# Two deformable-attention stages of one kernel rearranged: x placed by ScalarE, two-tap spreads from tap 12, ten accumulating DMAs, hats of one direction each

## The chip, the core and the metric

The kernel runs on one core of a Trainium2 chip. The time is device microseconds of one execution. The core has five engines that run their own instruction lists and wait for each other on semaphores: TensorE (PE, matmuls; its weight loads are PEld), VectorE (DVE), ScalarE (ACT), GpSimd (POOL) and SyncE (SP, which only issues DMAs here). ACT and POOL issue DMAs too, as ACTq and POOLq.

## What is computed

The input x is 4 images of 64 channels and 32x32 pixels, f32. The first part is deformable attention with 8 heads of 4 points. Each pixel has, for each head and point, an offset (two projections of x) and a weight (a softmax over the head's 4 points of a third projection). The projected values are sampled bilinearly at the shifted place, weighted, summed, projected and added to x:

```
q = x as tokens;  v = q @ W_value + b_value
off = q @ W_off + b_off;  attn = softmax(q @ W_attn + b_attn) over the points
loc = pixel + off;  sampled = bilinear(v, loc)            (0 outside the image)
x = sum over points(sampled * attn) @ W_out + b_out + q
```

The second part is a binary 3x3 convolution on the sign of x, a batch norm over the whole batch, a residual sum and a PReLU:

```
y = conv3x3(sign(x + move0), scale * sign(conv_w))
y = batchnorm(y) * gamma + beta + x + move1
out = where(y >= 0, y, a * y) + move2
```

## The kernel before

**Layout.** Two images of 64 channels fill the 128 partitions, so the four images are two groups g (`G` = 2). The pixels are split into an upper and a lower half, `yh` = 0 and 1, of 512 pixels (`HALF`). The attention works at a fixed grid of 4x4 integer shifts of the value image, the taps. Tap t of 0 to 31 is one shift in one half: taps 0 to 15 are the upper half, 16 to 31 the lower, and four taps with one y shift are a row. The order of the shifts is `ORDER`. (Where an offset reaches beyond the grid, a flag sends the engines to a general branch at the end; it isn't taken with these inputs.)

**Weights of a tap.** For every tap the weight of a pixel is attention times a hat in y times a hat in x, where a hat is relu(1 - |position - shift|). ScalarE makes the positions `u` (L644) from PSUM, then for each shift the distances `tab` (`distances`, L651) and the hats `hat` (`hats`, L656), in 8 steps n listed in `HATS`; one step has both directions, 1024 elements. VectorE multiplies attention, turned by TensorE into `ps_att`, with the y hat of a row: `attend(n)` (L862), into a ring `ays`. POOL multiplies that with the x hat for each tap: `weight(t)` (L785), into the ring `ap` of `RAP` = 4. Only taps 0 and 1 have it done by VectorE (L871).

**Spread, product, unit.** TensorE copies the weights of a tap's heads to the channels, `spread(t)`: one tap at a time up to tap 15 (L461), 8 instructions, and from `FIRST_PAIR` = 16 on two taps on half the rows each (L466), 16 instructions a pair. In a pair the second tap's output lands in swapped quadrants, and it is multiplied with `vswap`, a copy of the values `vpad` with swapped partitions, made by two DMAs on SP (L390). VectorE multiplies with the shifted values: `product(t)` (L888), into the ring `prod` of `PR` = 12. TensorE projects a product with W_out and accumulates it in `ps_out`: `project(unit)` (L490), 8 instructions. Two products can be added first by an accumulating DMA that POOL issues (`sum_products`, L792); `SUM_FROM` says which, e.g. 4: 5 means that product 5 is added onto product 4, and both are then one unit. It is issued four taps behind in POOL's order. There are 8 such sums, so 24 units. When a unit is projected is written out in `TAPS_AFTER` (after which spread which taps) and `TAPS_AT_END`. After the upper units (`UPPER_UNITS`) ScalarE reads `ps_out` (L706, L707) and the lower half uses the same banks.

**x itself** is added by matmuls with the identity into `ps_out` ahead of the units of each half: `carry_x(yh)` (L483). The second also holds the sum for the flag (L477).

**Softmax.** It runs in three parts: two halves of the upper pixels (parts 0 and 1) and all lower pixels (part 2): logits on TensorE (L429), `softmax_max`, `softmax_sub`, exponentials on ScalarE, `softmax_sum`, `softmax_recip` on VectorE, and the scale `prob`, for part 2 on POOL (L803) behind tap 7. `turn(1)` transposes it and only then can rows of the lower half be attended. On VectorE these steps stand between products; `ROW_AFTER` says after which products the rows 1 to 7 are attended.

**Start.** SP and ACT load x's upper half (one group each), then SP `win` (the projections) and ACT `prm` (biases, positions). SP waits for `win` and x and issues `cst` (hats' shifts, identity, selectors), the lower x, and the rest. TensorE runs three warm-up matmuls (L542), then biases of the logits (L419) and base positions (L408), which need `prm`, then logits (L429), offsets (L412) and values (L438).

**End.** After the last spread come the units at the end, with part of the convolution between (`convolve_above`, L524), the signs (L713), the rest of the convolution, the batch norm (L995 to L1016) and the stores.

## Time and profile before

| | |
|---|---|
| median of 3 runs | 95.33 us (94.48 to 97.89) |
| the profiled execution | 94.7 us, of which the span of the profile is 92.9 us |
| PE busy | 74.7 us (80% of the span) |
| DVE busy | 62.6 us (67%) |
| POOL busy | 51.7 us (56%) |
| ACT busy | 44.4 us (48%) |
| mean granted TensorE clock | 0.949 of full speed |

The span is from the first to the last instruction that the profiler recorded; 1.8 us of the execution lie outside it. Busy time of PE is the time in which at least one matmul runs, and matmuls overlap, so the duration of a group in the timeline is a little longer than the step to the next. The chain of waits gives those steps. A count (x8) is of instructions: an f32 matmul shows as two.

### The profile page before, as it was taken

To read this page: it belongs to the slowest core of one execution; us is meant where nothing else is said; L and a number is where in the kernel's file an instruction comes from. 1 tells how busy PE (TensorE), PEld (TensorE's weight loads), DVE (VectorE), ACT (ScalarE), POOL (GpSimd) and SP (SyncE) were. 2 spreads that over 40 slices of the span, in tenths; PEclk is the share of its full clock that TensorE was granted. 3 is DMA by queue.
4 is the path that set the end of the run, shared out by engine and by line. 5 is a ranking of instruction groups with operands and counts; after the bars stand their busy time and mean duration, and the time that the engine had idled before them with its cause. 6 is when DMAs were issued, how large, how long until landed. Compare 5 with 4: busy or idle time off the path is not lost.

```text
span 92.9 us, 1673 instructions
## 1 busy us (share of the span) xinstructions
PE 74.7 (80%) x642; PEld 30.2 (32%) x642; DVE 62.6 (67%) x85; ACT 44.4 (48%) x71; POOL 51.7 (56%) x48
## 2 busy tenths in 40 slices
PE   5669999669999999999999999969999999210000
PEld 4257529112335743333321313201313455010000
DVE  2000997993799874999897969799624007659930
ACT  2200399996399999970000799000000039419900
POOL 7920000019998999999999999999600000006000
PEclk9999999999999999999999999999999999995555
DMA  1839800000049938073290190697740000000085
GB/s 34 275 77 276 312 3 0 0 0 7 0 85 210 236 70 169 7 153 72 48 178 11 28 196 9 125 185 148 141 85 0 0 7 0 0 0 0 11 259 185
DMA packets 3641, 8.37 MB, mean 90 GB/s; under 512 B 560, under 2 KB 1072, under 8 KB 3632
## 3 DMA queue, kind: packets, MB, share of 16 engines
q0 software_dynamic: 1152, 4.19, 23.8%
q1 hardware_dynamic: 2192, 3.76, 13.7%
q10 hardware_dynamic: 288, 0.30, 1.1%
q8 instruction: 5, 0.08, 0.3%
q14 instruction: 4, 0.03, 0.1%
HBM read 2.27 MB, written 1.05 MB: 36 GB/s over the span
## 4 chain that ended last, share of the span: by engine, by line
PE 69%; DVE 9%; ACT 6%; DMA 4%; POOL 4%; issue 2%; ACTq 1%; POOLq 0%; DVEq 0%
PE banks L490 23%; PE banks L461 13%; PE banks L466 10%; DMA prm<-params_dram 4%; PE banks L412 4%; PE banks L483 4%; PE banks L419 3%; PE banks L524 3%; PE banks L429 3%; POOL ap L785 2%; ACT prod L765 2%; PE banks L438 2%; PE banks L408 2%; ACT prod L767 2%; DVE a L871 1%
## 5 line engine op out<-in xcount | busy, mean ns | idle before, releaser
L785 POOL TENSOR_TENSOR ap<-ays,hat 128x512 f32<-128x512 f32 x30 | 41.0, 1589 | 15.3 <-ACT hat L656 15.3
L888 DVE TENSOR_TENSOR prod<-banks,vpad 128x1024 f32<-128x1024 f32 (+1 forms) x26 | 30.2, 1175 | 9.1 <-PE banks L461 4.6
L490 PE MATMUL banks<-prod,wo 64*64 64x512 f32 x192 | 24.6, 598 | 0.2 <-PE banks L490 0.2
L461 PE MATMUL banks<-ap,cst 64*64 64x512 f32 x112 | 15.1, 593 | 0.0
L466 PE MATMUL banks<-ap,cst 32*64 32x512 f32 x128 | 12.1, 612 | 0.9 <-POOL ap L785 0.7
L490 PEld LDWEIGHTS banks<-prod,wo 64*64 64x64 f32 x192 | 7.6, 132 | 13.6 <-issue 11.5
L811 POOL TENSOR_SCALAR prod<-prod,prm,st 128x512 f32<-128x512 f32 x2 | 1.5, 767 | 18.0 <-ACT st L759 18.0
L713 ACT ACTIVATE sg<-banks,st 128x512 bf16<-128x512 f32 x2 | 1.3, 690 | 17.7 <-PE banks L490 17.7
L651 ACT ACTIVATE tab<-u,cst 128x1024 f32<-128x1024 f32 x8 | 8.9, 1141 | 0.2
L792 POOL DMA_DIRECT2D prod<-prod x8 | 8.6, 1078 | 0.1
L888 DVE TENSOR_TENSOR prod<-banks,vswap 128x1024 f32<-128x1024 f32 x7 | 8.5, 1215 | 0.0
L656 ACT ACTIVATE hat<-tab 128x1024 f32<-128x1024 f32 x8 | 8.2, 1048 | 0.1
L461 PEld LDWEIGHTS banks<-ap,cst 64*64 64x64 f32 x112 | 4.8, 132 | 7.6 <-issue 4.0
L466 PEld LDWEIGHTS banks<-ap,cst 32*64 32x64 f32 x128 | 2.7, 130 | 9.7 <-POOL ap L785 5.4
L862 DVE TENSOR_TENSOR ays<-banks,hat 128x512 f32<-128x512 f32 x8 | 5.4, 680 | 0.6 <-PE banks L446 0.6
L706 ACT ACTIVATE x1n<-banks,prm 128x512 f32<-128x512 f32 x1 | 0.7, 690 | 10.0 <-PE banks L490 10.0
L670 ACT ACTIVATE ex<-lsub 128x256 f32<-128x256 f32 (+1 forms) x3 | 1.5, 485 | 7.8 <-DVE lsub L826 7.8
L524 PE MATMUL banks<-sg,wcb 64*64 64x512 bf16 (+2 forms) x84 | 4.6, 350 | 0.2 <-ACT sg L713 0.2
L929 DVE TENSOR_SCALAR x<-banks,prm 128x512 f32<-128x512 f32 x1 | 0.8, 750 | 5.7 <-ACT sg L713 5.7
L429 PEld LDWEIGHTS banks<-win,xs 128*128 128x128 f32 x32 | 4.2, 201 | 0.9 <-issue 0.8
L419 PE MATMUL banks<-prm,top_ones 128*128 128x256 f32 (+1 forms) x6 | 3.2, 660 | 1.5 <-DMA prm<-params_dram 1.5
L820 DVE TENSOR_REDUCE lmax<-banks 128x64 f32<-128x256 f32 (+1 forms) x3 | 1.5, 510 | 3.8 <-PE banks L429 3.8
(83 smaller groups left out, 86.3 us busy)
## 6 DMA issues: line engine op xcount, KB each, us to landing
prod<-prod POOLq DMA_DIRECT2D x8, 512.0 KB, 4.9
xs<-x_dram SPq DMA_DIRECT2D x3, 256.0 KB, 4.0
vswap<-vpad SPq DMA_DIRECT2D x2, 361.0 KB, 5.6
out_dram<-prod SPq DMA_DIRECT2D x4, 128.0 KB, 2.5
out_dram<-prod SPq DMA_DIRECT2D x2, 256.0 KB, 2.5
wcf<-w_conv_dram SPq DMA_DIRECT2D x1, 288.0 KB, 4.1
wab<-w_abs_dram SPq DMA_DIRECT2D x1, 288.0 KB, 4.2
xs<-x_dram ACTq DMA_DIRECT2D x1, 256.0 KB, 3.4
```

Source lines behind the costliest of these rows:

```text
L419: pe.matmul(ps_log[part][:, first:end], top_ones[:], prm[:, p_att:p_att + HP].unsqueeze(1).to_broadcast([P, (end - first) // HP, HP]), sta ...
L429: mm = pe.matmul(ps_log[part][:, at:at + C], xs[:, g, q:q + P], wp[:, 2, :], start=False, stop=((n + 1) * P == end and g == G - 1), skip_g ...
L461: mm = pe.matmul(spread_into(t)[rows_out, g, :], sel_of(g)[rows_in, rows_out], weights_at(t)[rows_in], start=True, stop=True)
L466: mm = pe.matmul(spread_into(t)[quadrant(i, g, t in SWAPPED)[1], g, :], sel_of(g)[rows_in, quadrant(i, g)[1]], weights_at(t)[rows_in], sta ...
L490: mm = pe.matmul(ps_out[g][rows_out], wo[rows_in, rows_in], source[rows_in, g, :], start=False, stop=last, skip_group_check=True)
L524: mm = pe.matmul(ps_y[yh][g][rows_out, first_row * W:last_row * W], wcb[rows_in, ky * K + kx, :], sg[rows_in, g, y0:y0 + last_row - first_ ...
L651: nc.scalar.activation(tab[:, n % 2], u[:, :, yh, :], ACT.Abs, bias=cst[:, c_tap + k:c_tap + k + 1]).then_inc(s_abs, 1)
L656: nc.scalar.activation(hat[:, yh, :, k, :], tab[:, n % 2], ACT.Relu, bias=1.0, scale=-1.0).then_inc(s_hat, 1)
L785: pool.tensor_tensor(ap[:, j % RAP, :], ays[:, t // TAPS % RY, :], hat[:, yh, 0, kx, :], ALU.mult).then_inc(s_ap, 1)
L792: pool.dma_start(prod[:, into % PR], prod[:, more % PR], accum_op=ALU.add).then_inc(s_s2[k % len(s_s2)], 16)
L862: nc.vector.tensor_tensor(ays[:, n % RY, :], ps_att[:], hat[:, yh, 1, ORDER[row], :], ALU.mult).then_inc(s_ay, 1)
L888: nc.vector.tensor_tensor(by_half_row(prod[:, t % PR, g, :]), by_half_row(spread_into(t)[:, g, :]), v_window(t, g), ALU.mult).then_inc(s_p, 1)
```

## The change

- TensorE no longer adds x. ScalarE copies x into `ps_out` ahead of each half's units (`place_x`, four instructions of 512 elements); the sum for the flag is a step of its own behind the last units but one (`sum_flag`), and its ScalarE step stands just ahead of the last signs.
- Spreads of two taps begin at tap 12 instead of 16, so taps 13 and 15 use `vswap`; that copy is made in two halves, the first as soon as the upper values are there.
- Ten sums instead of eight. In the first three rows second onto first and fourth onto third product (0: 1, 2: 3, and so on), row 3 has none; the lower half is unchanged. They are issued five taps behind instead of four. Units are 22 instead of 24, and `TAPS_AFTER` is written anew.
- `distances` and `hats` work on one direction each, in 16 steps of 512 elements, in the order y of row 0, all x, the other y; `tab` has 4 places.
- `prm` is SP's first issue, `win` ACT's second. The y positions are projected first.
- The ring `ap` has 6 places instead of 4. Attention of the two halves has a bank each, and other banks are dealt out anew (`ps_log`, `ps_flag`, `ps_y`), which takes some waits away; TensorE's offsets of the lower half are split over the places behind tap 1 and tap 2, values behind tap 4, `turn(1)` behind tap 6.
- VectorE attends rows after products 0, 2, 4, 7, 8, 9, 10 and does `softmax_sum(2)` and `softmax_recip(2)` behind products 2 and 3. POOL's `prob` stands behind tap 5 instead of tap 7.

The core of the diff:

```diff
-FIRST_PAIR = NT
+FIRST_PAIR = 12
 SPREADS = [(t,) for t in range(FIRST_PAIR)] + [(t, t + 1) for t in range(FIRST_PAIR, LAST - 1, 2)] + [(LAST - 1,), (LAST,)]
 SWAPPED = [taps[1] for taps in SPREADS if len(taps) == 2]
-SUM_FROM = {0: 1, 4: 5, 8: 9, 12: 13, 16: 18, 20: 22, 21: 23, 24: 26}
+SUM_FROM = {0: 1, 2: 3, 4: 5, 6: 7, 8: 9, 10: 11, 16: 18, 20: 22, 21: 23, 24: 26}
+SUM_BEHIND = 5
 DVE_COLUMNS = [2] + [0] * (ROWS - 1)
 GPSIMD_LINES = (0, 1)
 ORDER = (1, 0, 2, 3)
-HATS = [(yh, k) for yh in range(YH) for k in ORDER]
+POSITIONS = [(yh, d) for yh in range(YH) for d in (1, 0)]
+HATS = [(0, 1, ORDER[0])] + [(0, 0, k) for k in ORDER] + [(0, 1, k) for k in ORDER[1:]]
+HATS += [(1, d, k) for d in (1, 0) for k in ORDER]
 VP = H + TAPS
 HW = W // 2
...
-        tab = sb("tab", [P, 2, 2, HALF])
+        tab = sb("tab", [P, 4, HALF])
...
-        RA, RAP = 3, 4
+        RA, RAP = 3, 6
...
-        ps_att = bank[6]
-        ps_y = [[bank[0], bank[1]], [bank[2], bank[3]]]
+        ps_att = [bank[6], bank[7]]
+        ps_y = [[bank[2], bank[3]], [bank[6], bank[7]]]
         ps_v = [[bank[0], bank[1]], [bank[5], bank[4]]]
...
-        ps_log = [bank[7], bank[6], bank[4]]
-        ps_flag = bank[4]
+        ps_log = [bank[7], bank[6], bank[7]]
+        ps_flag = bank[6]
...
-        def wait_for_hat(engine, yh, k):
-            engine.wait_ge(s_hat, HATS.index((yh, k)) + 1)
+        def wait_for_hat(engine, yh, d, k):
+            engine.wait_ge(s_hat, HATS.index((yh, d, k)) + 1)
...
-        TAPS_AFTER = {6: [2, 3], 7: [0], 8: [6], 9: [7], 10: [4], 12: [10], 13: [11], 14: [8], 17: [14, 15], 19: [12],
-                      23: [17, 19], 25: [16], 29: [20], 30: [21, 25], 31: [27, 29]}
+        TAPS_AFTER = {7: [0], 8: [2], 11: [4], 13: [6], 15: [8, 12], 17: [10, 14, 13, 15], 21: [17, 19],
+                      25: [16], 27: [25], 29: [20], 30: [21, 27], 31: [29]}
         TAPS_AT_END = [24, 28, 30, 31]
         UNITS_AFTER = {t: [unit_of(k) for k in TAPS_AFTER[t]] for t in TAPS_AFTER}
         UNITS_AT_END = [unit_of(t) for t in TAPS_AT_END]
         UNITS = [unit for t in UNITS_AFTER for unit in UNITS_AFTER[t]] + UNITS_AT_END
-        UPPER_UNITS = UNITS.index(unit_of(12)) + 1
...
         @block.sync
         def _(sp):
+            sp.dma_start(prm[:], params).then_inc(s_prm, 16)
             sp.dma_start(chunk(xs, 1, 0), chunk_of(x, 1, 0)).then_inc(s_x[0], 16)
-            sp.dma_start(win[:], w_in).then_inc(s_win, 16)
             sp.wait_ge(s_win, 16)
             sp.wait_ge(s_x[0], 32)
             sp.dma_start(cst[:, 0:c_avg], const[:, 0:c_avg]).then_inc(s_cst, 16)
...
-            sp.wait_ge(s_vp, 2)
-            sp.wait_ge(s_vlow, 2)
-            for i in range(PAIR):
-                rows_in, rows_out = quadrant(i, 1)
-                sp.dma_start(vswap[rows_out, :, RH + 1:], vpad[rows_in, :, RH + 1:]).then_inc(s_vswap, 16)
+            for yh in range(YH):
+                sp.wait_ge([s_vp, s_vlow][yh], 2)
+                at = slice(yh * VP // YH, (yh + 1) * VP // YH)
+                for i in range(PAIR):
+                    rows_in, rows_out = quadrant(i, 1)
+                    sp.dma_start(vswap[rows_out, :, at], vpad[rows_in, :, at]).then_inc(s_vswap[yh], 16)
...
-                        pe.wait_ge(s_f1, 1)
-                    for i in range(PAIR):
-                        rows_of_i = slice(i * C, (i + 1) * C)
-                        mm = pe.matmul(ps_out[g][rows_of_i], cst[rows_of_i, c_eye + i * C:c_eye + (i + 1) * C],
-                                       chunk(xs, g, yh)[rows_of_i], start=True, stop=False, skip_group_check=True)
-                mm.then_inc(s_carry, 1)
+            def sum_flag():
+
+                pe.wait_ge(s_ov, 4)
+                pe.wait_ge(s_p, products_done(LAST - 1, G - 1))
+                pe.matmul(ps_flag[0:1, 0:4], ones[:, 0:1], over_sum[:], start=True, stop=True).then_inc(s_fps, 1)
...
-                    pe.wait_ge(s_carry, 1)
+                    pe.wait_ge(s_xin, G)
                 if unit == UNITS[UPPER_UNITS]:
-                    pe.wait_ge(s_carry, 2)
+                    pe.wait_ge(s_xin, 2 * G)
                 last = unit in (UNITS[UPPER_UNITS - 1], UNITS[-1])
                 if kind == "sum":
                     wait_for_sum(pe, n)
...
             pe.wait_ge(s_x[0], 32)
             logits(0, range(NCH // 2))
             logits(1, range(NCH // 2, NCH))
+            offsets(0, 1)
             offsets(0, 0)
-            offsets(0, 1)
             values(0)
+            pe.wait_ge(s_sub, 2)
+            logits_bias(2)
             pe.wait_ge(s_x[1], 32)
-            pe.wait_ge(s_u, 2)
-            logits_bias(2)
             logits(2, range(NCH // 2))
             pe.wait_ge(s_cst, 16)
-            pe.wait_ge(s_sub, 2)
             turn(0)
             logits(2, range(NCH // 2, NCH))
+            pe.wait_ge(s_u, 2)
+            base_positions(1, 1)
             for taps in SPREADS:
                 for t in taps:
                     spread(t)
                 if t == 1:
-                    pe.wait_ge(s_sub, 3)
-                    for d in reversed(range(2)):
-                        base_positions(1, d)
-                        offsets(1, d)
-                if t == 3:
+                    offsets(1, 1)
+                if t == 2:
+                    base_positions(1, 0)
+                    offsets(1, 0)
+                if t == 4:
                     pe.wait_ge(s_u, 4)
                     values(1)
-                if t == TAPS + 1:
-                    carry_x(0)
-                if t == 2 * TAPS:
-                    pe.wait_ge(s_ay, TAPS)
+                if t == 6:
                     turn(1)
-                if t == FIRST_PAIR + 5:
-                    carry_x(1)
                 for unit in UNITS_AFTER.get(t, []):
                     project(unit)
             for unit in UNITS_AT_END[:-1]:
                 project(unit)
+            sum_flag()
             pe.wait_ge(s_p, products_done(LAST - 2, G - 1))
...
             pe.wait_ge(s_p, products_done(NT * YH - 1, G - 1))
+            pe.wait_ge(s_f1, 1)
             pe.wait_ge(s_sg, 4)
...
             act.dma_start(chunk(xs, 0, 0), chunk_of(x, 0, 0)).then_inc(s_x[0], 16)
-            act.dma_start(prm[:], params).then_inc(s_prm, 16)
-
...
             def distances(n):
-                yh, k = HATS[n]
-                act.wait_ge(s_u, 2 * yh + 2)
-                if n >= 2:
-                    act.wait_ge(s_hat, n - 1)
-                nc.scalar.activation(tab[:, n % 2], u[:, :, yh, :], ACT.Abs, bias=cst[:, c_tap + k:c_tap + k + 1]).then_inc(s_abs, 1)
+                yh, d, k = HATS[n]
+                act.wait_ge(s_u, POSITIONS.index((yh, d)) + 1)
+                if n >= 4:
+                    act.wait_ge(s_hat, n - 3)
+                nc.scalar.activation(tab[:, n % 4], u[:, d, yh, :], ACT.Abs, bias=cst[:, c_tap + k:c_tap + k + 1]).then_inc(s_abs, 1)
 
             def hats(n):
-                yh, k = HATS[n]
+                yh, d, k = HATS[n]
                 act.wait_ge(s_abs, n + 1)
-                nc.scalar.activation(hat[:, yh, :, k, :], tab[:, n % 2], ACT.Relu, bias=1.0, scale=-1.0).then_inc(s_hat, 1)
+                nc.scalar.activation(hat[:, yh, d, k, :], tab[:, n % 4], ACT.Relu, bias=1.0, scale=-1.0).then_inc(s_hat, 1)
+
+            def two_hats(n):
+                distances(n)
+                distances(n + 1)
+                hats(n)
+                hats(n + 1)
+
+            def place_x(g, yh):
+                nc.scalar.activation(ps_out[g][:], chunk(xs, g, yh), ACT.Identity).then_inc(s_xin, 1)
...
-            positions(0, 0, 1)
-            positions(0, 1, 2)
+            positions(0, 1)
+            positions(0, 0)
             act.wait_ge(s_cst, 16)
             distances(0)
+            distances(1)
             hats(0)
-            distances(1)
+            distances(2)
             hats(1)
-            distances(2)
-            distances(3)
             hats(2)
-            hats(3)
-            positions(1, 1, 3)
-            positions(1, 0, 4)
+            two_hats(3)
+            two_hats(5)
             exponentials(2)
+            positions(1, 1)
+            positions(1, 0)
+            distances(7)
+            hats(7)
             act.wait_ge(s_zero, 2)
             act.wait_ge(s_v, 2)
             for g in range(G):
                 nc.scalar.activation(values_of(g, 1), both_halves(ps_v[1][g][:]), ACT.Identity,
                                      bias=prm[:, p_bv:p_bv + 1]).then_inc(s_vlow, 1)
-            distances(4)
-            hats(4)
-            distances(5)
-            distances(6)
-            hats(5)
-            distances(7)
-            hats(6)
-            hats(7)
+            for g in reversed(range(G)):
+                act.wait_ge(s_vlow, G - g)
+                place_x(g, 0)
+            for n in range(8, len(HATS), 2):
+                two_hats(n)
             for n in range(2 * YH):
...
             nc.scalar.activation(chunk(x1, 0, 0), ps_out[0][:], ACT.Identity, bias=prm[:, p_bo:p_bo + 1]).then_inc(s_x1, 1)
-            act.wait_ge(s_fps, 1)
-            nc.scalar.activation(flag[:, 4:8], ps_flag[0:1, 0:4], ACT.Identity, accum_out=flag[:, 0:1]).then_inc(s_f1, 1)
+            act.wait_ge(s_x1, 2)
+            for g in reversed(range(G)):
+                place_x(g, 1)
...
+            act.wait_ge(s_fps, 1)
+            nc.scalar.activation(flag[:, 4:8], ps_flag[0:1, 0:4], ACT.Identity, accum_out=flag[:, 0:1]).then_inc(s_f1, 1)
...
             for t in range(TAPS, NT * YH):
                 weight(t)
                 for into in SUM_FROM:
-                    if SUM_FROM[into] == t - TAPS:
+                    if SUM_FROM[into] == t - SUM_BEHIND:
                         sum_products(into)
-                if t == 2 * TAPS - 1:
+                if t == TAPS + 1:
                     pool.wait_ge(s_rec, 3)
                     pool.tensor_tensor(grouped(prob[:, 1, :]), grouped(ex[:, 1, :]), spread_points(lrec[:, 1, :]),
                                        ALU.mult).then_inc(s_prob, 1)
...
-                wait_for_hat(dve, yh, ORDER[row])
-                nc.vector.tensor_tensor(ays[:, n % RY, :], ps_att[:], hat[:, yh, 1, ORDER[row], :], ALU.mult).then_inc(s_ay, 1)
+                wait_for_hat(dve, yh, 1, ORDER[row])
...
                 if t in SWAPPED:
-                    dve.wait_ge(s_vswap, 16 * PAIR)
+                    for half in range(YH):
+                        dve.wait_ge(s_vswap[half], 16 * PAIR)
...
             weight(0)
+            weight(1)
             softmax_max(2)
-            weight(1)
-            ROW_AFTER = [1, 3, 5, 9, 10, 12, 13]
+            ROW_AFTER = [0, 2, 4, 7, 8, 9, 10]
             for t in range(NT * YH):
                 product(t)
                 if t == 0:
                     softmax_sub(2)
+                if t == 2:
+                    softmax_sum(2)
                 if t == 3:
-                    softmax_sum(2)
-                if t == 4:
                     softmax_recip(2)
                 if t in ROW_AFTER:
                     n = ROW_AFTER.index(t) + 1

```

## Rows read from the trace of the kernel before

**Rows 1.** Chain of waits, start to 58.9 us: start, duration, engine, tile, line, instructions

```profile
1.17 4.14 DMA prm<-params_dram
...
5.44 2.05 PE banks L419 x4
7.49 0.85 PE banks L408 x2
8.34 1.83 PE banks L429 x16
10.17 1.87 PE banks L412 x8
...
13.05 1.06 PE banks L419 x2
...
22.67 1.88 PE banks L461 x16
...
58.86 0.04 POOLq L784
```

**Rows 2.** Busy time by stretch; after each engine (instructions); then clock, DMA share, GB/s

```profile
12.00:15.00 3.00, 3.00 (x22) 1.70 (x21) 2.83 (x7) 2.88 (x4) 0.00 (x0) 1.00 0.00 0
...
20.00:60.00 40.00, 40.00 (x356) 14.03 (x360) 33.32 (x34) 24.83 (x44) 38.94 (x35) 1.00 0.45 91
```

**Rows 3.** Timeline of POOL: start, duration, engine, line, operation, tiles, count, idle before

```profile
20.48 2.51 POOL L785 TENSOR_TENSOR ap<-ays,hat 128x512 f32<-128x512 f32 x2 [15.26 <-ACT hat L656]
...
29.37 1.10 POOL L803 TENSOR_TENSOR prob<-ex,lrec 128x512 f32<-128x512 f32 x1 [0.43 <-DVE lrec L839]
...
62.42 1.98 POOL L785 TENSOR_TENSOR ap<-ays,hat 128x512 f32<-128x512 f32 x1
63.64 1.60 POOL L792 DMA_DIRECT2D prod<-prod  x1
64.25 2.29 POOL L785 TENSOR_TENSOR ap<-ays,hat 128x512 f32<-128x512 f32 x1
```

**Rows 4.** Chain of waits, TensorE from 27 us to its last unit

```profile
27.35 1.72 PE banks L483 x8
...
39.26 1.72 PE banks L461 x16
...
49.13 1.04 PE banks L466 x16
...
52.86 1.86 PE banks L483 x8
...
66.35 1.88 PE banks L490 x16
...
71.31 2.81 PE banks L490 x24
...
75.69 0.02 issue
```

**Rows 5.** Timeline of TensorE, its first instructions

```profile
0.99 2.93 PE L542 MATMUL banks<-ones 128*128 128x256 f32 x6 [0.99 <-POOL ones L773]
```

**Rows 6.** Timeline of ScalarE: positions of the upper half, and the upper result

```profile
11.56 1.27 ACT L644 ACTIVATE u<-banks,prm 128x512 f32<-128x512 f32 x2
...
51.26 0.69 ACT L706 ACTIVATE x1n<-banks,prm 128x512 f32<-128x512 f32 x1 [10.04 <-PE banks L490]
```

**Rows 7.** Timeline of VectorE in the first rows

```profile
19.80 1.21 DVE L888 TENSOR_TENSOR prod<-banks,vpad 128x1024 f32<-128x1024 f32 x1
20.93 0.68 DVE L862 TENSOR_TENSOR ays<-banks,hat 128x512 f32<-128x512 f32 x1
...
28.35 0.94 DVE L839 RECIPROCAL lrec<-lsum 128x128 f32<-128x128 f32 x1
```

**Rows 8.** Accumulating DMA, issue to landing; then the stores to DRAM, last their us

```profile
DMA to landing us min/median/max: 4.6/4.9/5.7
...
out_dram<-prod SPq DMA_DIRECT2D x2, 256.0 KB, 2.5
```

26 lines of the change are left out of this document (10 added, 16 removed).

## The prediction

> **What bounds the kernel now.** I read the chain of waits first. It begins with the wait for `prm`, the last of four early transfers, and only then come TensorE's bias and position matmuls [rows 1]. From 22.7 to 58.9 us the chain is TensorE without a break [rows 1], so a reader may think that every matmul taken away is gained. The stretches by engine correct this: between 20 and 60 us PE is busy 40.00 of 40 us, but POOL 38.94 too [rows 2]. The timeline of POOL shows why it is no less a bound. Its products of weights (`weight`, L785) start every 1.23 us (two take 2.51 from 20.48, one 1.28), with no idle time noted but 15.26 us before the first, where it waits for a hat, and 0.43 before `prob` [rows 3]. Near the end the completions of taps 30 and 31 are 64.25+2.29 = 66.54 and 62.42+1.98 = 64.40, 2.14 apart, with one DMA issue between them: so an issue costs POOL 2.14-1.23 = 0.91 us. Sum of the before: 30 weights at 1.23 = 36.9, 8 issues at 0.91 = 7.3, `prob` 1.07, wait 0.43: 45.7 us; from 20.48 it ends at 66.2, measured 66.54. POOL is a machine at a constant rate and ends 1.7 us before PE begins `spread(31)`, behind the two units that take 1.88 from 66.35 [rows 4]. The two engines bound the kernel together, and what PE gives back is lost where POOL is late. Behind PE's last unit, which ends at 75.69 [rows 4], come signs, the rest of the convolution, the batch norm and the stores: 17.2 us that the change leaves as they are.
>
> All times below are in the clock of the profiled before. What the start gains is taken off at the end, since the first 15 us are one chain that shifts as a whole.
>
> **Start.** `prm` was ACT's second issue and landed at 5.31, 4.14 us after it; now it is SP's first. Bounds of its landing from issue: 2.5 us (a store of 128 to 256 KB on quiet queues [rows 8]) and 4.1 as now, so 3.2 to 4.9. I take the low end, as little runs ahead of it. PE's warm-up matmuls end at 3.92 [rows 5], so L419 starts at 3.9 and not 5.44: 1.5 us. `win` takes the slot that `prm` had, lands near 5.3 as that did, and is needed after L419 and L408 (2.05+0.85): at 6.8, hidden. `cst` and the lower x keep their places behind the same waits on SP and are wanted 1.5 us sooner: `cst` at 12.8-1.5 = 11.3, the lower x at 12.6. Both are ahead of four other loads, and from 12 us the DMA share is 0.00 [rows 2]: hidden. Gain 1.5, from 0.6 (4.9) up. What the clock adds stands with the rivals.
>
> **Hats and POOL's start.** ScalarE had 1024 elements per instruction; now 512, at a pitch of 0.6 (two `positions` in 1.27) [rows 6]. The hats start at 12.9, just behind them. POOL's first weight needs hat 3, the ninth instruction: 12.9+8x0.6+0.7 = 18.4, against 20.48. A gain of 2.1 us at first sight.
>
> **What is queued behind.** VectorE's `attend(1)` now stands straight behind `product(0)` and ahead of `product(1)`, and needs the y hat of row 1, hat 5, the thirteenth instruction: 12.9+12x0.6+0.7 = 20.8. Before, `product(1)` ran at 19.80 and the ays at 20.93. Now: `attend(1)` 20.8 to 21.5, then by pitches of 1.13 for a product (19.80 to 20.93) and 0.6 for an instruction of half its size product(1) 21.45, product(2) 22.6, sum 23.7, attend(2) 24.3, product(3) 24.9, reciprocal 26.05 and 0.94 long, ending at 27.0 [rows 7]. POOL meanwhile: taps 2 and 3 end at 20.9, tap 4 needs `attend(1)`, 21.5; tap 5 ends at 24.0. There stands `prob` (moved from behind tap 7 to behind tap 5), which needs that reciprocal: POOL waits 3.0 us where it waited 0.43, then prob ends at 28.15. Behind `prob` are queued all of POOL's other weights. TensorE no longer waits 0.70 for `lsub` (bank 7 in place of 4), but that frees PE at a place where POOL has nothing for it.
>
> **POOL's end.** 26 weights follow, and 9 issues: two sums more than before, less the last one (26 onto 24), which comes five taps late instead of four and so behind tap 31. 28.15+26x1.23+9x0.91 = 68.3, against 66.54. So the deeper ring (6) and the early hats don't bring POOL home earlier; it is 1.8 us later, and with the start's 1.5 off, 0.3.
>
> **TensorE.** Removed: two `carry_x`, 1.72 and 1.86; two units of 8 instructions at 0.94 (two took 1.88); four spreads of single taps at 0.86 (two in 1.72) become two pairs at 1.04: 1.4. In all 3.6+1.9+1.4 = 6.9 us [rows 4]. They go to waiting. `place_x` puts 4x0.6 us on ScalarE, which sat idle for 10 us before L706 [rows 6]: hidden. `turn(1)` comes near 30.5 and is wanted by `attend(4)` near 33.7; the upper half of `vswap` is copied from about 15 us, when no load runs any more [rows 2], and wanted by product 13 near 43: hidden, both. Units of early sums now wait for landings (4.9 us from issue [rows 8]): sum 0 is issued near 29 and lands near 34, sum 2, issued near 32.4, near 37.3, and PE stands between. It is behind POOL until the four units after tap 17 (done near 54.7), and from there catches up, spending some 1.0 per pair where POOL needs 2.5. Near the end: second half of (28,29) behind POOL's tap 29 at 65.8, to 66.4; unit 20 to 67.4; spread(30) 68.4; units 21 and 27 70.3; spread(31) 71.3; unit 29 72.3; draining for the change of quadrant 0.2: 72.5. Unit 24 is next and waits for the last sum. In before, tap 30 ended at 64.40 and that sum's issue, at 63.64, was 0.76 ahead of it [rows 3]; the same distance gives 68.3-0.76+4.9 = 72.4. Both are equal: 72.5. By the bounds 4.6 and 5.7 of landing it is 72.5 to 73.2.
>
> A rule of the Trainium skill stands against this row. Its page "DMA: Bandwidth & Descriptors", section "Anatomy of one DMA — SWDGE (gpsimd) path", gives about 2.0 us plus bytes over 436 GB/s for such a transfer, an estimate of 3.2 us for 512 KB. By it the last sum lands at 70.7 and only PE's order holds unit 24, at the same 72.5, and the early sums would hold nobody for long. The row has 4.9 with an accumulating write, and I go by the row.
>
> **Tail.** From unit 24 to the end of unit 31 was 75.69-71.31 = 4.38 [rows 4]; `sum_flag` adds one 4-column matmul, some 0.1; its short followers on ScalarE and VectorE start 1.6 us ahead of the signs and are hidden behind the convolution and unit 31. 72.5+4.4+0.1 = 77.0; less 1.5: 75.5, against 75.69. Sum: -0.2. Span 92.9-0.2 = 92.7, time 94.5 where the profiled run had 94.7. That run lies 0.6 under the median 95.33 and 0.2 over the fastest; I put the forecast between the two bases, at **94.8**.
>
> **Rivals.**
> A, 0.20: the stall before `prob` isn't there, as ScalarE and VectorE come through the first rows faster than I pitch them. POOL's work is then 30x1.23+9x0.91+1.1 = 46.2 from 18.4, ending 64.6; unit 24 follows its sum at 68.7 and the end is 73.2-1.5 = 71.7: 4.0 less, 90.8. Half of the stall gives 92.8. For it: TensorE has 6.9 us less to do. Against: `attend(1)` ahead of `product(1)`, and a reciprocal behind three more products.
> B, 0.15: the start gains more than 1.5, since the granted speed rises sooner. L419's four instructions of 256 columns took 2.05 at 5.44, and its two of 512 columns 1.06 at 13.05, half the time per column [rows 1]: so the clock got to the upper of its two levels (1.2 and 2.4 GHz) between them, by the even pace of L429 from 8.34 about 8 us in, after PE had worked from 5.44. The profile grants full speed from the start, which those rows don't bear out. Without the gap at 3.92 it may rise before L419, whose 2.05 and 0.85 would halve: 1.2 more, 93.6 on this base.
> C, slower, 0.17: the same clock the other way. PE gets to the logits at 6.8 with the clock still at the lower level. Sixteen at twice 0.114 are 1.8 more, eight of `offsets` at twice 0.234 another 1.9 [rows 1]. If it rises near 8, the price is 0.5; it decides if it rises later than about 10, when the whole 1.5 and half of `offsets` are gone: 94.8+1.5+1.0 = 97.3. For it: PE worked 0.99 to 3.92 without leaving the lower level. Against: no gap comes between.
> The Trainium skill ("TensorE: Matmul & The Clock Gate", section "Part 1: The HAM clock gate") has the low clock as the default and activity as what releases it; by that, work without a gap speaks for B.
> D, 0.48: my forecast, with own range 94.0 to 95.9 (gain at the start 0.6 to 1.9, landing up to 5.7).
>
> **How the numbers follow.** Faster by over 2% (under 93.1 us, as the base is 95.0; 2% is about what a measurement of this kernel tells from no change): A's 0.20 and a share of B, 0.24. Slower by over 2% (above 96.9): C's later half and landings beyond the bounds, 0.18. Within: 0.58. The range leaves out the full A and the far end of C: 92.6 to 96.9.
>
> **What would show it.** In the profile after: `prm` landed by 3.9 and L419 without idle time before it; `attend(1)` behind a wait for a hat, `product(1)` some 1.6 us later relative to product(0) than before; POOL idle about 3 us before `prob`, released by the reciprocal; tap 31 ending near 66.8; TensorE with idle time between 26 and 37 us, released by POOL and by the sums' DMAs; unit 24 starting near 71.0. If POOL's idle time is under 1 us, A holds and the forecast is wrong; if L429 starts later than 7.5, the start is.

## The result, and the profile after

The changed kernel took 97.27 us at the median of 4 runs (96.56 to 97.91), the kernel before 94.91. Some executions of a kernel are over 1.5% longer than its fastest one, those of the kernel before above all, and the ratio leaves them out: it is 1.036 with a 95% interval of 1.027 to 1.046, more than that of the two medians. So the change is slower by 3.6%, where 0.2% faster was forecast and 96.9 was the upper end of the range. The profiled execution took 97.51 us with a span of 95.7, 2.8 more than before.

The chain of waits of the changed kernel (start, duration, what) looks different from [rows 1] and [rows 4]. TensorE has no unbroken stretch any more; POOL, an accumulating DMA and gaps stand in it:

```profile
34.15 1.05 ACT hat L647 x2
...
35.23 2.14 POOL ap L787
...
39.53 6.91 DMA prod<-prod
46.44 0.04 issue
46.48 1.95 PE banks L483 x16
...
53.60 2.54 issue
...
67.79 5.93 DMA prod<-prod
73.72 0.04 issue
73.77 2.81 PE banks L483 x24
...
78.42 0.03 issue
```

L483 is the unit (L490 before), L465 and L470 are the spreads of one and two taps (L461, L466), L787 is POOL's weight (L785), L794 the accumulating DMA (L792), L891 VectorE's product (L888). The last unit ends at 78.42, against 75.69 [rows 4]: 2.73 later. All that follows is as long as before, so the loss of the profiled execution is made ahead of it.

The timeline of POOL (start, duration, engine, line, idle time before and its releaser at the end), to be held against [rows 3]:

```profile
16.39 2.53 POOL L787 TENSOR_TENSOR ap<-ays,hat 128x512 f32<-128x512 f32 x2 [11.16 <-ACT hat L647]
19.37 2.51 POOL L787 TENSOR_TENSOR ap<-ays,hat 128x512 f32<-128x512 f32 x2 [0.46 <-DVE ays L864]
24.82 1.10 POOL L805 TENSOR_TENSOR prob<-ex,lrec 128x512 f32<-128x512 f32 x1 [2.93 <-DVE lrec L841]
...
39.53 2.07 POOL L794 DMA_DIRECT2D prod<-prod  x1
40.14 3.98 POOL L787 TENSOR_TENSOR ap<-ays,hat 128x512 f32<-128x512 f32 x2
...
43.22 10.38 POOL L787 TENSOR_TENSOR ap<-ays,hat 128x512 f32<-128x512 f32 x7
56.15 0.88 POOL L794 DMA_DIRECT2D prod<-prod  x1 [2.56 <-DVE prod L891]
...
64.11 4.66 POOL L787 TENSOR_TENSOR ap<-ays,hat 128x512 f32<-128x512 f32 x3
67.79 1.82 POOL L794 DMA_DIRECT2D prod<-prod  x1
```

Tap 31 is complete at 64.11+4.66 = 68.77, against 66.54. The timelines account for the 2.23 us: start -4.09 (20.48 to 16.39), `attend(1)` +0.46, `prob` +2.50 (2.93 for 0.43), one issue more ahead of tap 31 +0.91, and a wait for product 18 ahead of the issue at 56.15, +2.56. The sum is +2.34. That is where POOL's time went; it doesn't say yet what caused it. Behind tap 31, unit 24 starts 5.00 later (4.77 before), and from there to the end are 4.65 (4.38 before): +0.5.

TensorE, from the units that wait for a sum onward:

```profile
43.65 1.38 PE L470 MATMUL banks<-ap,cst 32*64 32x512 f32 x16
46.48 1.95 PE L483 MATMUL banks<-prod,wo 64*64 64x512 f32 x16 [1.45 <-DMA prod<-prod]
48.36 1.11 PE L470 MATMUL banks<-ap,cst 32*64 32x512 f32 x16
49.40 1.95 PE L483 MATMUL banks<-prod,wo 64*64 64x512 f32 x16
51.53 1.95 PE L483 MATMUL banks<-prod,wo 64*64 64x512 f32 x16 [0.18 <-PE banks L483]
53.41 1.95 PE L470 MATMUL banks<-ap,cst 32*64 32x512 f32 x24
56.00 1.09 PE L470 MATMUL banks<-ap,cst 32*64 32x512 f32 x8 [0.65 <-DVE prod L891]
57.02 1.95 PE L483 MATMUL banks<-prod,wo 64*64 64x512 f32 x16
58.90 1.95 PE L470 MATMUL banks<-ap,cst 32*64 32x512 f32 x24
61.49 1.09 PE L470 MATMUL banks<-ap,cst 32*64 32x512 f32 x8 [0.65 <-DVE prod L891]
```

Two things are to be seen. TensorE stands idle ahead of units 8 and 12 (46.48) until sum 8 lands. And at 53.41 a pair of taps (18, 19) and half of the next (20) run together, but tap 21 has to wait for a bank until VectorE is through with product 18. A whole pair costs 1.04 [rows 4]; a split one costs 0.86 for its first tap, 0.65 of waiting and 1.02 for its second. That happens twice. VectorE stood idle for 2.69 us just before product 18, while TensorE went through four units:

```profile
54.63 1.23 DVE L891 TENSOR_TENSOR prod<-banks,vpad 128x1024 f32<-128x1024 f32 x1 [2.69 <-PE banks L470]
```

This is the product that POOL waits for at 56.15, and the one whose bank tap 21 needs. Behind it the two engines come to the end nearly together. The pair (28, 29) takes 1.57 us to the next unit instead of 1.04, since its second half starts at 66.37, as soon as POOL has tap 29 ready:

```profile
65.82 1.64 PE L470 MATMUL banks<-ap,cst 32*64 32x512 f32 x16
```

From there TensorE works without a break up to unit 24, which waits 0.36 more for the sum that POOL issued at 67.79. So by these rows POOL's lateness alone would give the end nearly as it is, and TensorE's alone would give one some 0.9 us sooner (0.53 at tap 29 and 0.36 at unit 24). The two lie beside each other, and the order of the units behind tap 17 stands ahead of both.

### The profile page after: what moved, and what is told of

Read it like the earlier page. It is cut to its first block, busy times and chain, and to the rows that moved or that the text cites. A ratio compares the mean times of both kernels' runs of the same rounds, so it can differ in the third digit from the quotient of the medians.

```text
span 95.7 us, 1648 instructions
## 1 busy us (share of the span) xinstructions
PE 71.9 (75%) x610; PEld 25.9 (27%) x610; DVE 64.3 (67%) x85; ACT 48.2 (50%) x91; POOL 53.5 (56%) x50
## 3 DMA queue, kind: packets, MB, share of 16 engines
HBM read 2.27 MB, written 1.05 MB: 35 GB/s over the span
## 4 chain that ended last, share of the span: by engine, by line
PE 33%; POOL 18%; ACT 16%; DMA 13%; issue 8%; DVE 5%; ACTq 1%; POOLq 0%; DVEq 0%
POOL ap L787 15%; DMA prod<-prod 13%; PE banks L483 6%; PE banks L465 5%; ACT tab L642 5%; PE banks L416 4%; POOL prod L794 4%; PE banks L517 3%; ACT hat L647 3%; PE banks L423 3%; PE banks L535 3%; PE banks L433 3%; ACT prod L767 2%; PE banks L442 2%; ACT prod L769 1%
## 5 line engine op out<-in xcount | busy, mean ns | idle before, releaser
L787 POOL TENSOR_TENSOR ap<-ays,hat 128x512 f32<-128x512 f32 x30 | 43.6, 2110 | 11.6 <-ACT hat L647 11.2
L891 DVE TENSOR_TENSOR prod<-banks,vpad 128x1024 f32<-128x1024 f32 (+1 forms) x24 | 28.0, 1174 | 13.3 <-PE banks L470 8.1
L483 PE MATMUL banks<-prod,wo 64*64 64x512 f32 x176 | 22.3, 604 | 4.3 <-DMA prod<-prod 4.1
L794 POOL DMA_DIRECT2D prod<-prod x10 | 15.2, 1518 | 2.6 <-DVE prod L891 2.6
L470 PE MATMUL banks<-ap,cst 32*64 32x512 f32 x160 | 15.1, 609 | 1.7 <-DVE prod L891 1.3
L465 PE MATMUL banks<-ap,cst 64*64 64x512 f32 x80 | 11.6, 659 | 3.2 <-POOL ap L787 2.1
L483 PEld LDWEIGHTS banks<-prod,wo 64*64 64x64 f32 x176 | 5.6, 132 | 19.6 <-DMA prod<-prod 9.5
L891 DVE TENSOR_TENSOR prod<-banks,vswap 128x1024 f32<-128x1024 f32 x9 | 10.9, 1215 | 0.0
L642 ACT ACTIVATE tab<-u,cst 128x512 f32<-128x512 f32 x16 | 10.7, 713 | 0.0
L647 ACT ACTIVATE hat<-tab 128x512 f32<-128x512 f32 x16 | 9.2, 619 | 0.0
L470 PEld LDWEIGHTS banks<-ap,cst 32*64 32x64 f32 x160 | 4.0, 130 | 12.2 <-POOL ap L787 6.6
L465 PEld LDWEIGHTS banks<-ap,cst 64*64 64x64 f32 x80 | 2.7, 145 | 10.2 <-issue 6.4
L433 PEld LDWEIGHTS banks<-win,xs 128*128 128x128 f32 x32 | 4.1, 197 | 0.9 <-issue 0.8
L416 PE MATMUL banks<-xs,win 128*64 128x512 f32 x16 | 4.1, 611 | 0.0
L433 PE MATMUL banks<-win,xs 128*128 128x64 f32 x32 | 3.9, 271 | 0.0
L535 PE MATMUL banks<-ones 128*128 128x256 f32 x6 | 2.9, 661 | 1.0 <-POOL ones L775 1.0
```

The source lines that it names most:

```text
L416: mm = pe.matmul(ps_off[yh][d][g * C:(g + 1) * C, :], wp[:, d, :], chunk(xs, g, yh), start=False, stop=True, skip_group_check=True)
L433: mm = pe.matmul(ps_log[part][:, at:at + C], xs[:, g, q:q + P], wp[:, 2, :], start=False, stop=((n + 1) * P == end and g == G - 1), skip_g ...
L465: mm = pe.matmul(spread_into(t)[rows_out, g, :], sel_of(g)[rows_in, rows_out], weights_at(t)[rows_in], start=True, stop=True)
L470: mm = pe.matmul(spread_into(t)[quadrant(i, g, t in SWAPPED)[1], g, :], sel_of(g)[rows_in, quadrant(i, g)[1]], weights_at(t)[rows_in], sta ...
L483: mm = pe.matmul(ps_out[g][rows_out], wo[rows_in, rows_in], source[rows_in, g, :], start=False, stop=last, skip_group_check=True)
L535: pe.matmul(bank[6][:, 0:2 * P], ones[:], ones[:].unsqueeze(1).to_broadcast([P, 2, P]), start=True, stop=True)
```

## The experiments

Each kernel is timed with the kernel before on the same chip, which scattered from 93.1 to 99.1 us. So a ratio stands only where there is one on record; the others are compared with the changed kernel (97.27 us, and 97.46 when it was run again beside the last ones) and with each other. Most kernels ran on another chip than the changed one, and the ratios give larger gains than the medians (3.4% and not 2.2% for the second kernel below), so a gain against the changed kernel is good to about 1 us. The theories: 1, POOL's list ends last and its waits are the loss. 2, TensorE is late behind landings. 3, TensorE is late by the order of its own units. Where an expectation numbers its theories in another way, as the second and third do, its own words count.

**One issue of POOL moved.**

```diff
+ISSUED_BEHIND = {into: more + SUM_BEHIND for into, more in SUM_FROM.items()}
+ISSUED_BEHIND[16] = 26
-                      25: [16], 27: [25],
+                      27: [16, 25],
-                    if SUM_FROM[into] == t - SUM_BEHIND:
+                    if ISSUED_BEHIND[into] == t:
```

> The changed kernel with one DMA moved: POOL issues the sum of 18 onto 16 behind tap 26 instead of tap 23, and TensorE projects unit 16 behind tap 27 instead of 25. Theory 1 (POOL's list is what ends last, and its 2.56 us wait for product 18 at 53.6 us came on top of it): POOL doesn't wait there, tap 31 is complete near 66.2 instead of 68.8, and the span is 93.1, 2.5 less. Theory 2 (TensorE is late by itself behind the landing of sum 8, and POOL's wait only mirrors that): POOL's wait goes, but TensorE keeps its times, and the span stays at 95.7 with the last sum not waited for.

97.91 us, ratio to before 1.036 (1.027 to 1.045): nothing gained. The timeline of POOL shows waits of another name where the 2.56 us were:

```profile
53.65 3.75 POOL L789 TENSOR_TENSOR ap<-ays,hat 128x512 f32<-128x512 f32 x3 [0.79 <-PE banks L472]
57.34 0.87 POOL L796 DMA_DIRECT2D prod<-prod  x1
57.95 1.57 POOL L789 TENSOR_TENSOR ap<-ays,hat 128x512 f32<-128x512 f32 x1
60.60 0.88 POOL L796 DMA_DIRECT2D prod<-prod  x1 [1.09 <-DVE prod L893]
```

POOL now waits 0.79 for a spread and 1.09 for a later product, 1.88 in all and for TensorE or what follows it. Tap 31 is complete at 67.38 (68.77 before the edit; 0.72 of the difference is a sooner start), no landing is waited for ahead of unit 24, and the time is no better. So POOL's wait alone is not the loss, as theory 1 would have it; it mirrored a late TensorE. The test isn't clean, however. With unit 16 moved, three pairs of spreads stand in TensorE's list without a unit between, and there it lost time that it had not lost before:

```profile
60.45 3.35 PE L472 MATMUL banks<-ap,cst 32*64 32x512 f32 x24 [0.65 <-DVE prod L893]
```

From tap 22 to the pair (28, 29), with units 16 and 25, it took 8.19 us where the changed kernel took 6.92 (58.90 to 65.82). What POOL's wait costs with TensorE's list as it was is not shown.

**The scaling of the lower half behind tap 7 again.**

```diff
-                if t == TAPS + 1:
+                if t == 2 * TAPS - 1:
                     pool.wait_ge(s_rec, 3)
-                if t == 6:
+                if t == 7:
                     turn(1)
```

> The changed kernel with POOL's scaling of the lower half behind tap 7 again (and its transposition on TensorE behind tap 7 instead of 6). Theory 1: POOL's wait of 2.93 us for the reciprocal is gone or under 0.5, but its wait for product 18 grows if product 18 doesn't come earlier with it; the end moves by between -2.5 and 0. Theory 2 (the pile of accumulating DMAs sets TensorE's times): the first sums are issued 2.7 us sooner and land sooner, product 18 comes sooner by as much, and the span is 93.1. Theory 3 (the lower rows' attention comes too late instead): a new wait of VectorE for the transposition, span 95.7 or more.

95.14 us, ratio 1.001 (0.995 to 1.007): 2.1 us less than the changed kernel. POOL's wait of 2.93 us is gone and it issues the sums of the first rows sooner. The wait for product 18 (at 54.08) keeps its size, but product 18 comes 2.1 us sooner, as the second theory of the expectation has it:

```profile
24.93 1.37 POOL L805 TENSOR_TENSOR prob<-ex,lrec 128x512 f32<-128x512 f32 x1
...
38.60 0.88 POOL L794 DMA_DIRECT2D prod<-prod  x1 [0.96 <-DVE prod L891]
...
54.08 0.88 POOL L794 DMA_DIRECT2D prod<-prod  x1 [2.51 <-DVE prod L891]
```

**Three of the six upper sums left out.**

```diff
-SUM_FROM = {0: 1, 2: 3, 4: 5, 6: 7, 8: 9, 10: 11, 16: 18, ...
+SUM_FROM = {0: 1, 4: 5, 8: 9, 16: 18, ...
-        TAPS_AFTER = {7: [0], 8: [2], 11: [4], 13: [6], 15: [8, 12], 17: [10, 14, 13, 15], 21: [17, 19],
+        TAPS_AFTER = {6: [2, 3], 7: [0], 8: [6], 9: [7], 11: [4], 13: [10, 11], 15: [8, 12], 17: [14, 13, 15], 21: [17, 19],
```

> The changed kernel with the sums 3 onto 2, 7 onto 6 and 11 onto 10 left out: seven accumulating DMAs, 25 units instead of 22. TensorE has 3 units more (2.8 us). Theory 1 (pile-up: a landing takes 5.6 at the median and up to 6.9 us because the sums come every 3.07 us in the first rows): landings return to 4.6 to 5.2, TensorE doesn't wait 1.45 us for sum 8, POOL's wait for product 18 falls to under 1, and POOL has 3x0.91 less to issue: tap 31 near 64 to 65, span 92 to 93.5. Theory 2 (the units saved were worth their time): TensorE's 2.8 us more show, span 96 or more.

94.39 us, ratio 0.994 (0.989 to 1.000): 2.9 us less than the changed kernel, with 2.8 us more of matmuls. TensorE waits for unit 0's landing, and for another only near the end (0.48 ahead of unit 21); units 8 and 12 start without idle time at 43.58:

```profile
32.06 1.09 PE L483 MATMUL banks<-prod,wo 64*64 64x512 f32 x8 [1.17 <-DMA prod<-prod]
...
43.58 1.95 PE L483 MATMUL banks<-prod,wo 64*64 64x512 f32 x16
...
52.24 1.09 PE L470 MATMUL banks<-ap,cst 32*64 32x512 f32 x8 [0.65 <-DVE prod L891]
```

The landing itself fell less than the pile-up theory of the expectation said: 4.8/5.1/6.4 us (least, median, most) against 4.9/5.6/6.9. POOL still waits 2.17 us for product 18. So the extra sums cost time, and something else makes product 18 late. A third way in which they may cost isn't ruled out: TensorE's granted clock falls once in the middle of every profile of a kernel with ten sums and of none with seven (see the last section).

**The load order alone, in the kernel before.**

```diff
+            sp.dma_start(prm[:], params).then_inc(s_prm, 16)
             sp.dma_start(chunk(xs, 1, 0), chunk_of(x, 1, 0)).then_inc(s_x[0], 16)
-            sp.dma_start(win[:], w_in).then_inc(s_win, 16)
-            act.dma_start(prm[:], params).then_inc(s_prm, 16)
+            act.dma_start(win[:], w_in).then_inc(s_win, 16)
```

> The kernel before with only the first four loads in the order of the changed one (the params first on SP, the input weights second on ACT). If the start is a chain that shifts as a whole: logits begin at 6.5 instead of 8.1, POOL's first tap at 18.8 instead of 20.5, and the span is 91.2, 1.7 less. If something else holds the middle (the lower half of x, constants), less than 0.5.

92.93 us, ratio 0.982 (0.975 to 0.990), span 90.6: a gain of some 1.8%, near the 1.7 us expected. The profiled span fell by more, 2.3, and POOL's first tap came at 18.03 where 18.8 was expected, since the bias matmuls ran faster than in the profile before (2.05 us for the same four):

```profile
3.72 1.37 PE L419 MATMUL banks<-prm,top_ones 128*128 128x256 f32 x4
5.40 0.59 PE L408 MATMUL banks<-pos_b,ones_b 128*128 128x512 bf16 x2 [0.31 <-DVE pos_b L900]
```

All the rest of the change together costs some 4.3 us (97.27 less 92.93).

**The upper half's last units spread out.**

```diff
-        ... 17: [10, 14, 13, 15], 21: [17, 19],
+        ... 17: [10, 14], 19: [13, 15], 23: [17, 19],
```

> The changed kernel with the upper half's last units spread out as before: units 10 and 14 behind tap 17, 13 and 15 behind tap 19, 17 and 19 behind tap 23 (instead of four behind 17 and two behind 21). Theory 3: with two pairs of spreads back to back after four units, the second pair is split, since its second tap's bank waits for product 18; a split pair costs 1.88 plus 0.65 of waiting instead of 1.04, twice, so TensorE loses 3 us. With a unit between the pairs (18,19) and (20,21) the first split goes: product 18 about 1.9 us sooner, POOL's wait for it under 1, span 94.2 (1.5 less) or, if that wait counts as well, 93.2. Theory 2 (landing of sum 8 alone): span stays at 95.7, as no sum lands sooner.

95.66 us (95.40 to 96.36), 1.6 less than the changed kernel's first timing. By the spans of two profiles that start alike, 93.5 and 94.6 of the changed kernel run again, it is 1.1. TensorE's pair (20, 21) is no longer stopped, though the one behind it still is:

```profile
51.06 1.11 PE L470 MATMUL banks<-ap,cst 32*64 32x512 f32 x16
52.11 1.95 PE L483 MATMUL banks<-prod,wo 64*64 64x512 f32 x16
53.98 1.95 PE L470 MATMUL banks<-ap,cst 32*64 32x512 f32 x24
56.58 1.09 PE L470 MATMUL banks<-ap,cst 32*64 32x512 f32 x8 [0.65 <-DVE prod L891]
```

POOL's wait for product 18 fell from 2.56 to 0.92. No transfer was touched, only the order of four units, so the order costs time by itself, as theory 3 says. The run doesn't divide the gain between the split that went (some 1.5) and product 18, which has two units behind tap 17 ahead of it instead of four and so releases POOL sooner.

**The units spread out and the scaling behind tap 7** (both edits above).

> The changed kernel with both: units spread out as in a_space, and the scaling of the lower half behind tap 7. If the gains are independent, the 3.4% that the scaling's place gave and what a_space gives add up: span 92.3 or less. If both act through product 18, no more than the larger of the two.

93.69 us (93.14 to 94.11), span 92.3: 3.6 less than the changed kernel, where the two alone gave 1.6 and 2.1. They add up.

**Seven sums and the scaling behind tap 7** (both edits above).

> The changed kernel with seven sums (three upper ones left out) and the scaling behind tap 7. Each alone gave 4.0 and 3.4% against the changed kernel. If they are independent (one the DMAs' pile, the other POOL's 2.9 us of waiting), span near 89.8; if both only bring units of the first rows sooner to TensorE, near 92.

91.46 us (91.01 to 91.62), span 89.6: 5.8 less than the changed kernel, where the two alone gave 2.9 and 2.1. They add up and somewhat more, as far as the chips can be compared.

**x placed by ScalarE, in the kernel before with the new load order.** The edit takes `carry_x` out of TensorE's list and puts `place_x` and `sum_flag` in, as in the change; all other parts stay but the bank of the flag's sum.

> The kernel before with the new order of loads, and x placed by ScalarE instead of TensorE's matmuls (3.6 us of TensorE less); all the rest as before: no new pairs, eight sums, hats of both directions. Against the run with the loads alone (span 90.6, POOL's tap 31 complete at 64.11, TensorE's spread of it at 65.7): if TensorE's time counts up to where POOL holds it, the end comes 1.5 us sooner, span 89.1. If the upper result is late behind the four copies on ScalarE, 90.6 or more. If TensorE was the only bound, 3.6 less, 87.0.

93.11 us (92.42 to 93.56) and span 90.6, where the load order alone had 92.93 and 90.6. The 3.6 us of TensorE's time are worth nothing by themselves in that kernel, not even the 1.5 that I expected. TensorE near tap 28, first without and then with the carry matmuls taken out:

```profile
59.57 2.31 PE L466 MATMUL banks<-ap,cst 32*64 32x512 f32 x16 [0.74 <-POOL ap L785]
```

```profile
59.35 2.31 PE L466 MATMUL banks<-ap,cst 32*64 32x512 f32 x16 [1.05 <-POOL ap L781]
```

It waits 0.31 longer for POOL and starts 0.22 sooner, and its list from there on is the same. Where the second carry had stood between two pairs, one pair is split here too.

**The changed kernel again**, beside the next two.

> The changed kernel as it is, on the same chip as the next two, so that they can be compared with it: 97.3 us, and the same order of waits (sum 8 waited for by TensorE, product 18 by POOL).

97.46 us (96.38 to 97.89), span of the profiled one 94.6, of which 0.67 is a sooner start: POOL's first tap at 15.72 instead of 16.39. POOL waits 2.28 us for product 18, TensorE is split twice. But in the fourth row sum 8 is in time here, and sum 10 is what TensorE waits for, 0.69. Which landing is late changes from run to run.

**All ten sums, but the units later.**

```diff
-        TAPS_AFTER = {7: [0], 8: [2], 11: [4], 13: [6], 15: [8, 12], 17: [10, 14, 13, 15], 21: [17, 19],
+        TAPS_AFTER = {9: [0], 11: [2], 13: [4], 15: [6, 12], 17: [8, 14], 19: [10, 13, 15], 23: [17, 19],
```

> The changed kernel with all ten sums, issued by POOL as before, but each unit of the upper half two taps later in TensorE's list (unit 0 behind tap 9, 2 behind 11, and so on to 8 and 14 behind 17; 10, 13 and 15 behind 19; 17 and 19 behind 23), and two more semaphores for the sums. It takes away TensorE's waits for landings and nothing of POOL's work. Against a_space (span 93.5, units spread out but not later): if TensorE's idle time behind the landings is what the extra sums cost, 1.34 us at 49.2 and 2.34 at 32.2 go and the span is 91 to 92. If POOL's 3x0.91 us of issues are the cost, 93.5 stays. If the later units pile up at the end of the half, up to 95.

The edit also gives the sums two more semaphores. 94.26 us (93.96 to 94.72), span 92.3; against the kernel with the units spread out 1.4 us less, 1.2 of the span, where 1.5 to 2.5 of the span were expected. TensorE waits for no landing up to unit 24, though the landings are as long as ever, 5.2/6.1/6.5 us. POOL's wait for product 18 (0.92 there) is gone with it. So TensorE's idle time behind landings, with what it makes late, costs some 1.4 us. The rest of what leaving out sums gained may be POOL's issues or the granted clock; neither was taken alone.

**Three together: seven sums, the scaling behind tap 7, the units spread out.**

> The changed kernel with three things together: seven sums, the scaling of the lower half behind tap 7, and the upper half's last units spread out (14 behind tap 17, 13 and 15 behind 19, 17 and 19 behind 23). The first two together had a span of 89.6, with POOL waiting 2.46 us for product 18 and two split pairs. If the spreading takes one split and most of that wait as it did in a_space: 88.1. If the end is by now TensorE's plain work: 89.0 or more.

90.04 us (89.62 to 90.28), span 87.8, against 97.46 and 94.6 of the changed kernel on that chip, 4.9 us under the median of the kernel before (94.91) and 3.1 under the fastest of its runs beside it (93.14). It is faster than both kernels. POOL's wait for product 18 is 0.55, TensorE has one split left:

```profile
44.89 1.62 PE L470 MATMUL banks<-ap,cst 32*64 32x512 f32 x16
46.44 1.95 PE L483 MATMUL banks<-prod,wo 64*64 64x512 f32 x16
48.32 1.95 PE L470 MATMUL banks<-ap,cst 32*64 32x512 f32 x24
50.91 1.09 PE L470 MATMUL banks<-ap,cst 32*64 32x512 f32 x8 [0.65 <-DVE prod L891]
```

Everything else of the change is in it (hats of one direction, x by ScalarE, pairs from tap 12, the ring of six, the load order). Against the load order alone (92.93) it is some 2.9 us faster, with one sum fewer than the kernel before.

## Why the prediction was wrong, step by step

**Start: right.** L423 began at 3.83 for 3.9, the logits at 6.52 for 6.8, `attend(0)` 1.72 sooner for 1.5. The run with the load order alone confirms the gain, by ratio. Rival C didn't happen: sixteen of L433 took 1.73 from 6.71, at the pace that they had before. Rival B didn't happen in this profile, where L423 took 1.95, as at the lower level. But it is part of what happens: in nine of the twelve profiles with the new load order the same four instructions took 1.22 to 1.81 us (2.04 here, in the timeline) and the two of L412 0.59 (1.05 here), so the clock had risen by then, and the logits began at 5.83 to 5.88. In the same kernel run again this made the start 0.64 us sooner, about half of B's price of 1.2.

**Hats, `attend(1)` and the stall before `prob`: right.** POOL began at 16.39 for 16.9 (18.4 less 1.5); the rows of VectorE and the wait of 2.93 us for 3.0 came as walked, and `prob` ended at 25.92 for 26.65. Putting `prob` behind tap 7 again gave back 2.1 us. Rival A falls with it.

**POOL's end: failed, by a wait that I put at nothing.** The step counted 26 weights and 9 issues from `prob` to 68.3, as if POOL waited for nobody. But an issue waits for its second product, and the issue of sum 16 waited 2.56 us for product 18. My own walk had that product too late for the issue (spread near 55 in the clock of before, so the product near 57, and the issue near 56), and I didn't lay the two side by side. From `prob` to tap 31 POOL took 42.85 for the 40.15 of the forecast, and tap 31 was complete at 68.77 for 66.8. The run with that issue moved shows that the wait was not the whole cause: TensorE was late as well.

**TensorE: failed in the same place.** Up to there it was in time: the four units after tap 17 were done at 53.41 for 53.2 (54.7 less 1.5). I wrote that from there it "catches up, spending some 1.0 per pair". It doesn't catch up, because a pair costs 1.04 only if both banks are free. With three banks for spreads and four units in a row behind tap 17, VectorE runs dry, then the second pair needs the bank of product 18, which VectorE has just begun. A split costs 0.86+0.65+1.02 = 2.53 instead of 1.04, two of them 3.0 us; TensorE was through with the pair (28, 29) at 67.39 where the forecast had 64.9. That the end was forecast 2.9 too early is near these 3.0, but it is no proof: at tap 29 TensorE waited for POOL once more, so POOL's 2.56 and TensorE's 3.0 don't add. In the kernel before, a unit or a carry stood between all pairs but the last two, so this cost is not in [rows 4] at all. Spreading the units took one split and most of POOL's wait and gave 1.6 us. One split is left in every run, so its price is worked out and not measured.

**Landings: mis-sized.** I took 4.9, the median, and a bound of 5.7 from [rows 8]. In the kernel before, the first six sums, 5.5 to 7.5 us apart, took 4.6 to 5.0, but the last two, 1.8 and 4.3 behind their neighbours, took 5.7 and 5.3. The last is the one that counts, so 4.9 was too low even for the old order. The ten sums of the changed kernel showed 4.9/5.6/6.9, its first six, at one in some 3.07 us, 5.1 to 6.9:

```profile
DMA to landing us min/median/max: 4.9/5.6/6.9
```

The last sum was issued at 67.79 for 66.0 and took 5.93 for 4.9, so unit 24 started at 73.77 where 71.0 was forecast; by TensorE's list alone it would have been about 73.4. By the run with later units the landings ahead of TensorE cost some 1.4 us. The rule of the Trainium skill ("DMA: Bandwidth & Descriptors", section "Anatomy of one DMA — SWDGE (gpsimd) path"), an estimate of 3.2 us, is further off than the row: no accumulating DMA in these profiles landed in less than 4.5.

**Tail: near.** 4.65 for 4.5.

**The 6.9 us of TensorE: right that they go to waiting,** and the run with x by ScalarE alone shows it for 3.6 of them. But the forecast then should have asked what TensorE's idle time does to the order of the rest.

So what failed is the stretch from tap 18 on. The order of the units there makes product 18 late, and POOL's wait for it (2.56) and TensorE's split pairs (1.5 each) were both put at nothing. The run with later units shows that the cause lies there and in the landings: with all ten sums and all other parts of the change, and only the units spread out and two taps later, the time was 94.26, where 94.8 had been forecast (some 0.7 of it by the sooner start). How the loss divides between the two engines is argued from the rows.

Against the load order alone the changed kernel loses some 4.3 us. The undone parts give back 2.1 (place of `prob`), 2.9 (three sums) and 1.6 (order of units), and together 7.2 (97.27 less 90.04), which is 2.9 more than the loss; by the spans of the two profiles that start alike it is 6.8. What is open: how the 2.9 of the sums divides between TensorE's waits, POOL's issues and the clock, how the 1.6 of the order divides between the split and POOL, and what each of the other parts gains alone.

## What to carry to other kernels

When a list of one engine is rearranged, lay each of its instructions against the moment when its buffer comes free, not only against its input: a group of units without a spread between starves the next engine, and the pairs behind it then pay. A wait that stands at the engine that looks like the bound can be the mirror of another's lateness. Moving the waiting instruction is a test of that, if the other engine's list stays as it was. What uses a transfer that was added to save a matmul must stand in the list as late as the transfer lands under the new load, not under the old one.

## What the runs showed of the hardware

TensorE's granted clock fell in the middle of the kernel, where it never did before. Busy time by stretch of the changed kernel (after each engine its instructions in brackets, then clock, DMA share, GB/s):

```profile
20.00:30.00 10.00, 7.42 (x48) 2.09 (x44) 8.29 (x10) 8.26 (x15) 7.07 (x7) 0.85 0.37 84
30.00:40.00 10.00, 7.12 (x62) 2.26 (x64) 6.49 (x8) 9.90 (x20) 10.00 (x11) 0.98 0.89 170
```

and one of its spreads in that stretch:

```profile
27.20 1.98 PE L465 MATMUL banks<-ap,cst 64*64 64x512 f32 x8 [2.09 <-POOL ap L787]
```

Eight instructions took 1.98 us, the pace of the lower level (1.2 GHz), where eight of the same line took 1.09 at 24.02, at the upper level (2.4 GHz); ahead of them TensorE had idled 2.09. The best kernel, with TensorE busy 8.74 and 9.66 us in the same two stretches, kept the upper level through both:

```profile
20.00:30.00 10.00, 8.74 (x76) 2.95 (x77) 8.99 (x10) 8.68 (x16) 10.00 (x10) 1.00 0.57 124
```

That agrees with the Trainium skill ("TensorE: Matmul & The Clock Gate", section "Part 1: The HAM clock gate"), by which the low clock is the default and activity releases it. The fall moved from run to run (0.85 in 20 to 30 us here, 0.83 in 30 to 40 in the second profile).

It stands once in each of the seven profiles of kernels with ten sums, and in none of the three with seven. What it costs was not measured by itself. One hint is in the ten executions of the kernel with three sums left out: two with a mean granted clock of 0.939 and 0.954 took 93.33 and 94.09 us, the other eight, at 0.912 to 0.929, took 93.98 to 95.65. So most of its executions seem to have had the fall that its profile lacks, and it may be worth half a microsecond; the two groups overlap.

POOL's record of an issue grew with the pace: 1.01 us for the first and 2.34 for the sixth at one in 3.07 us. A landing is counted from the start of that record, so part of the 6.91 us may have passed while POOL hadn't yet worked off the issue. In the kernel before the first was 1.00 and none over 1.60.
